# Self-attention by half sequences, with 64-row score matmuls and a later transpose, in a decoder of six layers

## The reference

```python
DIM, H, KV, HD, WIN = (128, 16, 4, 64, 64)
# xn = layernorm(x); q = rmsnorm(xn @ wq.T) (16 heads), k = rmsnorm(xn @ wk.T), v = xn @ wv.T (4 heads)
# scores = q @ k.T * HD ** -0.5, kept where 0 <= i - j < WIN; x = x + softmax(scores) @ v @ wo.T
```

## Time and profile before

| | before |
|---|---|
| median of 3 runs | 2810.6 us (2810.01 to 2815.29) |
| the profiled execution | 2811.5 us |
| its span | 2809.7 us |
| busy: PE, DVE, ACT, POOL | 2401.2, 2138.4, 1455.2, 1191.9 us |
| the self-attention layer | 1755.1 to 2271.3 us of the span |

### The profile page before, as it was taken

One profiled execution on the slowest core, in us unless ns is written; L12 is line 12 of the kernel. 1 busy time (PEld: TensorE's weight loads), 2 busy tenths in 40 slices (PEclk: granted clock), 3 DMA queues, 4 the chain that ended last, 5 costly groups with the idle time before them and its releaser, 6 DMA issues. The chain is left out here.

```text
span 2809.7 us, 46598 instructions
## 1 busy us (share of the span) xinstructions
PE 2401.2 (85%) x14880; PEld 1568.5 (56%) x14880; DVE 2138.4 (76%) x3085; ACT 1455.2 (52%) x2617; POOL 1191.9 (42%) x864
## 2 busy tenths in 40 slices
PE   2778878778887877799779999699999989978997
PEld 0233333333333332577578888466666767767776
DVE  3899999999999999577555555588888867764555
ACT  2666666666666774466332222466666646642010
POOL 4566667666666667333300000455555533231000
PEclk9899999999999999899789999899999999988999
DMA  2000000000000000200000000000000010000000
GB/s 84 1 0 0 1 0 1 1 1 0 0 0 0 0 1 0 63 12 12 22 1 1 1 0 0 6 0 0 0 0 0 1 48 11 11 4 1 11 7 12
DMA packets 35414, 22.17 MB, mean 8 GB/s; under 512 B 22710, under 2 KB 34017, under 8 KB 34801
## 3 DMA queue, kind: packets, MB, share of 16 engines
q1 hardware_dynamic: 35312, 20.98, 2.9%
HBM read 18.87 MB, written 2.10 MB: 7 GB/s over the span
## 5 line engine op out<-in xcount | busy, mean ns | idle before, releaser
L784 POOL TENSOR_TENSOR m_hc<-m_h,m_cs 128x1024 f32<-128x1024 f32 x256 | 603.2, 2359 | 351.9 <-DVE m_h L706 344.6
L706 DVE TENSOR_TENSOR_SCAN m_h<-m_da,m_pdb 128x1024 f32<-128x1024 f32 x256 | 585.1, 2286 | 23.5 <-DVE m_pdb L661 5.0
L456 PE MATMUL m_py<-m_hc,ident 128*128 128x512 f32 x1024 | 514.6, 627 | 4.2 <-DVE m_y L670 2.1
L579 ACT ACTIVATE m_da<-m_dt,m_aneg 128x508 f32<-128x508 f32 x512 | 337.8, 709 | 47.8 <-POOL m_dt L753 46.1
L661 DVE TENSOR_TENSOR m_pdb<-m_du,m_pdb 128x1024 f32<-128x1024 f32 x256 | 314.8, 1230 | 42.7 <-POOL m_du L760 11.4
L456 PEld LDWEIGHTS m_py<-m_hc,ident 128*128 128x128 f32 x1024 | 202.2, 200 | 213.6 <-issue 174.6
L594 ACT ACTIVATE m_cs<-m_pc 128x512 f32<-128x512 f32 x256 | 150.5, 588 | 219.7 <-PE m_pc L446 219.6
L442 PE MATMUL m_pdb<-m_bcrow,m_sel 96*128 96x512 bf16 x256 | 101.8, 397 | 171.8 <-DVE m_h L706 170.8
L1391 ACT ACTIVATE c_act_of<-c_pg 128x512 f32<-128x512 f32 x144 | 86.2, 598 | 237.3 <-PE c_pg L212 237.3
L1759 POOL TENSOR_TENSOR d_pr<-d_pr,d_rden 128x512 f32<-128x512 f32 x128 | 133.3, 1041 | 177.2 <-DVE d_rden L1690 177.2
L1037 ACT ACTIVATE x_prT<-x_pt 77x512 f32<-77x512 f32 x256 | 137.8, 587 | 130.6 <-PE x_pt L939 129.5
(11 more groups left out here) (257 smaller groups left out, 5373.7 us busy)
## 6 DMA issues: line engine op xcount, KB each, us to landing
cw_gu<-in_C_gu SPq DMA_DIRECT2D x1, 2304.0 KB
x<-in_x SPq DMA_DIRECT2D x8, 256.0 KB, 4.9
fw_w<-in_F_w SPq DMA_DIRECT2D x1, 2048.0 KB
out_x<-x SPq DMA_DIRECT2D x8, 256.0 KB, 2.3
bm_mrow<-in_B_mrow SPq DMA_DIRECT2D x1, 1232.0 KB, 6.5
x_ctxT<-in_B_ctxT SPq DMA_DIRECT2D x32, 38.5 KB, 1.8
x_mask<-in_B_mrow SPq DMA_DIRECT2D x32, 38.5 KB, 2.8
x_ctxT<-in_E_ctxT SPq DMA_DIRECT2D x32, 38.5 KB, 1.8
```

Source lines behind the costliest of these rows:

```text
L456: ins = mm(py[:, c, :], S.ident[:, :], hc[n % BUF][:, place(n, c), :], start=n == 0, stop=n == NS - 1)
L579: A_(dst, src, ACT.Exp, scale=aneg[:, d, c, n:n + 1]).then_inc(s["da_ready"], 1)
L706: V.tensor_tensor_scan(h[n % BUF][:, way], da[n % BUF][:, d:d + CH * GT][:, way], pdb[:, b:b + 2, :].rearrange("p c t -> p (c t)")[:, way] ...
L784: P.tensor_tensor(hc[n % BUF][:, :, :], h[n % BUF][:, :].rearrange("p (c t) -> p c t", c=CH), bc(cs[n % BUF][:, :], 1, CH), ALU.mult).then ...
```

## The change

The unit of work is half a sequence (8 heads) in place of a quad; the engines walk by `walk_halves`, `slot(u)` for each half u.

- `scores` writes the two-bank `ps` [128, 2, 4, 128] in one go: two mask matmuls, then 8 matmuls of 128 columns whose operands are 64 rows each, alternately rows 0 to 63 (bank 0) and 64 to 127 (bank 1). `kT` has no zeros any more. There is no second `ps`: the next half's scores wait for this half's subtraction.
- Maximum, subtraction, sum and reciprocal work on 8 heads (1024 elements), the maximum and subtraction of u ahead of the sum and reciprocal of u-1. Exponential and normalization work on 1024 elements too.
- `turn(u-3)` transposes 8 heads through the one bank `pt` in two parts, `values(u-4)` stands right behind it. At PE the scores of u+1 come last in a slot.
- q, k, v of a sequence are turned (`turn_kq`), the next sequence projected (`project_in`) and the last but one projected out in the second half's slot, in this order.
- The sum of squares, mean and power are made in two parts (12 and 8 heads). The copy of v goes from DVE to POOL. Mean and variance come from DVE's bn_aggr, the reciprocal deviation from POOL, one sequence at a time.
- The residual addition is the first thing on DVE in the first half's slot.

```diff
-def walk_halves(eng, slot, ahead):
+def walk_halves(eng, slot, ahead, behind=1):
...
-        kT = [A.sb(f"kT{p}", [128, KVL, 2, T]) for p in range(2)]
-        top, den, rden = ([A.sb(f"{n}{q}", [128, QH]) for q in range(NQ)] for n in ("top", "den", "rden"))
-        pr = [A.sb(f"pr{q}", [128, QH, T]) for q in range(NQ)]
-        prT = [A.sb(f"prT{q}", [128, QH, T]) for q in range(2)]
+        kT = [A.sb(f"kT{p}", [128, KVL, T]) for p in range(2)]
+        top, den, rden = ([A.sb(f"{n}{h}", [128, H2]) for h in range(2)] for n in ("top", "den", "rden"))
+        pr = [[A.sb(f"pr{p}{h}", [128, H2, T]) for h in range(2)] for p in range(2)]
+        prT = [[A.sb(f"prT{h}{k}", [128, QH, T]) for k in range(2)] for h in range(2)]
...
-        ps = [A.ps(f"ps{k}", [128, QH, T]) for k in range(2)]
+        ps = A.ps("ps", [128, 2, QH, T])
...
+                def turn(u):
+                    pe.wait_ge(s["norm_ready"], u.k + 1)
+                    for k in range(2):
+                        if due(2 * u.k + k):
+                            pe.wait_ge(s["prT_ready"], 2 * u.k + k)
+                        for i in range(QH):
+                            ins = tr(pt[:, i, :], pr[u.p][u.h][:, QH * k + i, :], S.ident[:, :])
+                        ins.then_inc(s["pt_mm"], 1)
+                def scores(u):
+                    if u.h == 0:
+                        pe.wait_ge(s["kT_ready"], u.n + 1)
+                    pe.wait_ge(s["qT_ready"], u.k + 1)
+                    if due(u.k):
+                        pe.wait_ge(s["sub_ready"], u.k)
+                    for k in range(2):
+                        mm(ps[:, k, :, :], S.ident_bf[:, :], bc(outside[:, :], 1, QH), start=True, stop=False)
+                    for i in range(QH):
+                        for k in range(2):
+                            half = slice(64 * k, 64 * k + 64)
+                            ins = mm(ps[:, k, i, :], qT[u.p][half, QH * u.h + i, :],
+                                     kT[u.p][half, 2 * u.h + i // 2, :], start=False, stop=i == QH - 1)
+                    ins.then_inc(s["s_mm"], 1)
...
+                def project_in(b):
+                    pe.wait_ge(s["xT_ready"], b.n + 1)
+                    if due(b.n):
+                        pe.wait_ge(s["kT_ready"], b.n)
+                    mm(pkv[:, :], xT[:, :], W.wkv[:, :], start=True, stop=True).then_inc(s["qkv_mm"], 1)
...
+                def slot(u):
+                    o, m, n = u.seq.plus(-2), u.seq.plus(1), u.seq.plus(2)
+                    if u.plus(-3).real():
+                        turn(u.plus(-3))
+                    if u.plus(-4).real():
+                        values(u.plus(-4))
+                    if u.h == 0 and n.real():
+                        turn_x(n)
+                    if u.h == 1:
+                        if m.real():
+                            turn_kq(m)
+                        if n.real():
+                            project_in(n)
+                        if o.real():
+                            project_out(o, n)
+                    if u.plus(1).real():
+                        scores(u.plus(1))
...
+                def slot(u):
+                    d = u.plus(-1)
+                    m, n, o = u.seq.plus(1), u.seq.plus(3), u.seq.plus(-3)
+                    if u.h == 0 and o.real():
+                        i = bass.ds(o.n, 1)
+                        dve.wait_ge(s["o_mm"], o.n + 1)
+                        V.tensor_tensor(S.x[:, i, :], S.x[:, i, :], bc(px[:, T:2 * T], 1, 1), ALU.add
+                                        ).then_inc(s["x_ready"], 1)
...
+                    if u.real():
+                        sc = ps[:, :, :, :].rearrange("p k i t -> p (k i) t")
+                        dve.wait_ge(s["s_mm"], u.k + 1)
...
+                        V.tensor_reduce(top[u.h][:, :], sc, AX.X, ALU.max).then_inc(s["top_ready"], 1)
+                        dve.wait_ge(s["top_ready"], u.k + 1)
...
+                        V.tensor_tensor(pr[u.p][u.h][:, :, :], sc, bc(top[u.h][:, :], 2, T), ALU.subtract
+                                        ).then_inc(s["sub_ready"], 1)
+                    if d.real():
+                        dve.wait_ge(s["exp_ready"], d.k + 1)
...
+                        V.tensor_reduce(den[d.h][:, :], pr[d.p][d.h][:, :, :], AX.X, ALU.add
+                                        ).then_inc(s["den_ready"], 1)
```

More of the change, by code:

```diff
@@ L818, in both @@
                 slot(Half(j, p, h))
-    for j in range(-turns, 1):
+    for j in range(-turns, behind):
         both(j)
-    with eng.Fori(1, NB // 2 - turns) as j:
+    with eng.Fori(behind, NB // 2 - turns) as j:
         both(j)
-    for j in range(NB // 2 - turns, NB // 2 + 1):
+    for j in range(NB // 2 - turns, NB // 2 + behind):
         both(j)
@@ L1542, in slot @@
[L1542 to L1581, removed]
-                        if n.real():
[L1583 to L1589, removed]
@@ new lines, in values @@
+                def values(u):
+                    pe.wait_ge(s["prT_ready"], 2 * (u.k + 1))
+                    if u.h == 0:
+                        pe.wait_ge(s["v_ready"], u.n + 1)
+                    if due(u.k):
+                        pe.wait_ge(s["cT_ready"], u.k)
+                    for e in range(2):
+                        for k in range(2):
+                            ins = mm(py[64 * k:64 * k + 64, e, :], v[u.p][:, 2 * u.h + e, :],
+                                     prT[u.h][k][:, 2 * e:2 * e + 2, :], start=True, stop=True)
+                    ins.then_inc(s["y_mm"], 1)
@@ L1593, in _ @@
+                walk_halves(pe, slot, 3, 2)
             @block.scalar
@@ L1596, in _ @@
                 act.wait_ge(s["kscale"], 2)
-                act.wait_ge(s["kT_zero"], 2)
-                def slot(b, q):
-                    y = b if q >= 2 else b.plus(-1)
+                def slot(u):
+                    e, t, y = u.plus(-1), u.plus(-3), u.plus(-4)
+                    m, n = u.seq.plus(1), u.seq.plus(2)
+                    if e.real():
+                        act.wait_ge(s["sub_ready"], e.k + 1)
+                        buf = pr[e.p][e.h]
+                        A_(buf[:, :, :], buf[:, :, :], ACT.Exp).then_inc(s["exp_ready"], 1)
+                    if t.real():
+                        for k in range(2):
+                            act.wait_ge(s["pt_mm"], 2 * t.k + k + 1)
+                            if k == 0 and due(t.k - 1):
+                                act.wait_ge(s["y_mm"], t.k - 1)
+                            A_(prT[t.h][k][:, :, :], pt[:, :, :], ACT.Copy).then_inc(s["prT_ready"], 1)
@@ L1747, in _ @@
+                walk_halves(dve, slot, 3, 2)
             @block.gpsimd
@@ L1749, in _, with slot @@
                 P = nc.gpsimd
-                for part, cols in enumerate(LN_PARTS):
-                    S.ln_scalars(pool, s["rstd"], LN_EPS, cols, part * LN_STEPS)
-                def slot(b, q):
-                    d = b if q < 3 else b.plus(1)
+                P.memset(one[:, :], 1.0).then_inc(s["one_ready"], 1)
+                pool.wait_ge(s["one_ready"], 1)
+                def slot(u):
+                    d = u.plus(-1)
+                    m, r4 = u.seq.plus(1), u.seq.plus(4)
+                    if u.h == 0 and m.real():
+                        for k in range(2):
+                            pool.wait_ge(s["ms_ready"], 2 * m.n + k + 1)
+                            if k == 0 and due(m.n):
+                                pool.wait_ge(s["kn_ready"], m.n)
+                            if due(2 * (m.n - 1) + k + 1):
+                                pool.wait_ge(s["qn_ready"], 2 * (m.n - 1) + k + 1)
+                            P.tensor_tensor(r[:, PARTS[k]], mean_sq[:, PARTS[k]], S.minus_half[:, PARTS[k]], ALU.pow
+                                            ).then_inc(s["r_ready"], 1)
@@ L1772, in _ @@
-                walk_sequences(pool, slot, 3)
+                    if u.h == 1 and u.real():
+                        pool.wait_ge(s["v_early_ready"], u.n + 1)
+                        if due(2 * (u.n - 1)):
+                            pool.wait_ge(s["y_mm"], 2 * (u.n - 1))
+                        P.tensor_tensor(v[u.p][:, :, :], v_early[u.p][:, :, :],
+                                        one[:, :].unsqueeze(2).to_broadcast([128, KVL, HDL]), ALU.mult
+                                        ).then_inc(s["v_ready"], 1)
```

289 lines of the change are left out of this document (130 added, 159 removed).

## The result

| | before | after |
|---|---|---|
| median, 4 runs of each on one chip | 2812.9 us (2810.0 to 2815.6) | 2841.2 us (2839.9 to 2842.1) |
| the profiled execution and its span | 2811.5, 2809.7 us | 2842.1, 2840.4 us |
| the self-attention layer in it | 516.1 us | 543.0 us (1759.1 to 2302.1) |

The ratio is 1.0100, with a 95% interval of 1.0083 to 1.0118: slower by 28 us, where +14 was forecast. The layer itself has 26.9 us of the 30.7 between the two spans. The other 4 lie ahead of it, in layers that are the same: this profile enters the layer at 1759.1 us, that of before at 1755.1. The ten profiles of this study enter it between 1753.9 and 1759.1, so this is a spread from run to run.

A forecast was written before the change was run, and what follows sets the result against it. A loop of DVE's stretch from output projection to subtraction and PE's path was taken to set a 15.9 us period; 27 steps +26, filling -16, end +4 made +14 on 2811.5, less 0.9: 2825 us, range 2804 to 2846.

The forecast's parts named there:

- three waits per sequence: PE waits for ACT's copy in each half's transposes (0.8 to 0.9 us) and DVE's subtraction before the second half's masks (0.8).
- Period: Time per sequence in the self-attention layer's middle: 15.9 us, between 15.6 and 16.2, against 14.95 before; 27 steps give +26 us.
- Sum 15.1 us: PE's work for one sequence, including two waits for ACT's copies and about 0.1 for the copy of k: 15.1 us.
- so I take 0.8 us: PE's wait for DVE's first-half subtraction: 0.9 us by the rows, taken as 0.8, between 0.5 and 1.1.
- DVE's stretch: DVE's ordered work from the output projection's end through the first half's subtraction, which frees `ps`: 5.5 us against PE's 4.6.
- The first rival: DVE's stretch does not bind, being below 4.6 us; PE alone sets 15.1 us per sequence: 2798 us, chance 0.13.
- The copy waits: Between the two parts of a half's transposes PE idles for ACT's copy of `pt`: 0.9 us per half.
- Filling: Time before the layer's first residual addition: 59 us with the start, 16 less than before; 12 less with more half-clock time.
- about 3.5 us less: At the layer's start one of POOL's ten norm operations, which ended at 4.8 us, remains ahead: about 3.5 us less.
- End: Emptying of the layer: the last two to three sequences pay dearer transposes and values, 1.5 us each more: +4 us.
- Scores: PE's two masks and eight 64-row matmuls of a half, with the 64-row pairs overlapping: 1.62 us.
- The rival of the clock: PE's clock falls to a mean of 0.9 in the layer's middle: 27 x 1.2 = +32, 2857 us, chance 0.08.

The follow-up runs named there:

- the first experiment: Changed kernel with the values of the half before placed between the two parts of a half's transposes on PE: 2837.0 us, ratio 1.0081 to the kernel before.

## Why the prediction was right in its direction and wrong in its size

Its direction and its mechanism held: three waits per sequence, at the places named, with the clock full in the middle. Its size did not: +14 against +28. By its own steps:

- **Period: 15.9 forecast, 16.26 measured; 27 x 0.36 = 10 of the 14 us that the forecast is short.** This is the step that failed, and both terms of it came out too small.
  - The larger is PE's own path, "Sum 15.1 us". PE's second slot has no slack, so each tenth in it counts 27 times. The terms give 1.62 + 1.95 + 1.01 + 1.41 + 2.58 + 1.79 = 10.36 us for it; masks to masks it took 10.61 and 10.69 by turns. In the sequence shown (2022.72 to 33.41) the transposes with their wait took 2.01, q and k with the wait for ACT's copy of k 1.60, the in-projection 2.65. The wait for the copy of k, put down as 0.1, was 0.2 to 0.3.
  - The smaller is "so I take 0.8 us". The rows gave a wait of 0.9; the discount for the gaps of 0.25 had no row. Measured in the sequence shown (masks at 2022.72, and 0.16 after the transpose of x they could have started) it is 0.98 us, in the one before 0.9.
- **DVE's stretch: 5.5 us forecast, 5.53 measured** from the projection's end to the masks. The sum is right by luck: both sums of squares with their gaps took 1.99 us where 2.19 was put down, maximum and subtraction with their hand-overs 2.73 where it was 2.55.
- **PE's own path in its own order is 15.4 us**, as the run with the later addition shows; the forecast 15.1 is 0.3 short. The 15.12 us of the run with the output projection first are no confirmation: that is another order, in which PE doesn't wait for the copy of k (q and k take 1.37 us) and the in-projection takes 2.58. The first rival needed a stretch below 4.6 us; it was 5.5.
- **That the stretch binds** is shown from four sides: shortening it by the addition (-0.81 us per sequence), starting it sooner (-1.13, the copy of k included), lengthening it (+1.4 at full clock), and relieving PE instead, which left the first half's slot at 5.70 us.
- **The copy waits** were priced at 0.9 us each; the rows show 0.69 and 0.77 of idle matmul queue, and 1.34 and 1.43 us from first to second part where 1.37 was forecast. The first half's is hidden in the changed kernel beside DVE's stretch, as the first experiment shows.
- **Filling: -16 forecast, -12.7 measured.** It came out near the 12 that was given for more half-clock time, though there is no more of it: a mean clock of 0.78 in 62.9 us and of 0.82 in 75.6 both come to some 27 us at half clock (62.9 x 0.22 x 2). Half of the miss is the start. With "about 3.5 us less" the first normalization would stand 1.3 us after the layer's start; it stands 3.0 after it, behind DVE's mean and variance of the other 28 sequences:

```profile
1760.02 1.94 DVE L1666 BATCH_NORM_AGGREGATE d_mv<-bn 128x2 f32<-128x6 f32 x28
...
1762.09 0.34 DVE L1746 TENSOR_SCALAR d_xh<-x,d_mv,rstd 128x128 f32<-128x128 f32 x1
```

  The first round ends 8.7 us after the start, where 6.3 was forecast. The others, by the ends of q's projection on PE (1767.8, 1778.5, 1790.1, 1806.6) and the first addition, took 10.7, 11.6, 16.5 and 15.4 us where 8.5, 14, 15 and 16 were forecast: each is off, but their sum only by 0.7.
- **End: +4, measured +4.1. Scores: 1.62 us, measured 1.62.** The 64-row pairs overlap as the 32-row strips of the earlier trace rows do.
- **Elsewhere: nothing forecast.** The median's difference is 28.3 us, the layer's 26.9.
- **The rival of the clock** did not come in the changed kernel, and came in three of its variants. Two expectations were missed with its help, and of the largest miss of all (some 58 us, the sum ahead of the maximum) 54 are the clock's.

## What to carry to other kernels

When one engine's work is cut and another's order sets a stretch in the same loop, sum both loops, take the waits inside a slot without slack (here for the copy of k) from rows, and give no discount to the loop that rows show; then ask which operation heads the stretch and whether its producer can stand sooner. Here the change lost 1%, and swapping two blocks in PE's program turned it into a gain of 0.3%, and one more move made that 1%. A cover that is removed (here scores between two uses of one bank) is found by asking, for every wait, what stood in it before. An edit can win next to nothing alone (0.14 us per sequence, with the clock's share) and 0.86 together with another, so the moves are tried in pairs.

## What was not expected of the hardware

- DVE's normalization of 128x128 elements took 0.34 us before the change and 1.75 us after it, in the time of POOL's product of 1024 columns; moved away from it, it took 0.34 again. In the timeline above it starts at 2029.89 and ends at 2031.70, and POOL's row beside it is this one; DVE is done 0.08 us after POOL:

```profile
2029.72 1.90 POOL L1772 TENSOR_TENSOR d_pr<-d_pr,d_rden 128x1024 f32<-128x1024 f32 x1 [3.80 <-DVE d_rden L1738]
```

  The Trainium skill (SBUF — State Buffer, section "SBUF: two separate sides") says that GpSimd and some DVE operations take one pair of ports as an exclusive lock, held for the whole instruction, while the other blocks; the trace agrees in that DVE's operation starts 0.17 us after POOL's product and is done just behind it. Not every operation of DVE is held up so: the products `kn` and `qn`, beside POOL's product that starts at 2024.02, took 0.69 and 1.28 us, as before the change.
- The granted clock fell to its lower level, 1.2 GHz, in regular, short stretches: 3.4 us in 65 with waits of 1.7 and 0.5 us per sequence, 6.8 us in 20.5 with one of 2.2 and two of 0.7 to 0.8, 3.4 us in 37.5 with one of 1.7 and three of 0.7 to 0.8; not with three of 0.7 to 0.8 alone, in the changed kernel. The first and the last of these have PE busy 86% alike. What in the pattern decides isn't settled.
- POOL's power took 2.28 us for 12 numbers and 1.64 for 8, 3.92 in all, against 3.54 for 20 at once: parting it costs little. Its product of 1024 columns 1.90 us against two of 1.04.
